# q and k in two float32r parts, paired heads in 64-row groups of TensorE, late maximum tiles by half the keys

## The chip, the cores and the metric

The kernel runs on one core of a Trainium2 chip. The metric is the device time of one launch in microseconds (us), here the median of three runs.

## The reference

Input is x of shape (4, 1024, 128) and float32 weights. Three residual steps follow each other:

```python
x = x + 0.5 * ffn(layernorm(x))       # router over 8 experts, one expert per token, 128 -> 512 -> 128, relu
x = x + attention(layernorm(x))
x = x + 0.5 * ffn(layernorm(x))
# attention: 16 heads of 8 numbers each, causal, 1024 keys
q, k, v = split_heads(x @ Wq.T), split_heads(x @ Wk.T), split_heads(x @ Wv.T)   # (64, 1024, 8)
q, k = rope(q, pos), rope(k, pos)
score = einsum('bqd,bkd->bqk', q, k); score = where(causal, score, -inf)
out = einsum('bqk,bkd->bqd', softmax(score / sqrt(8)), v) @ Wo.T
```

The output is (4, 1024, 128) float32. The change concerns q, k and the scores alone.

## The kernel before, in words

There are two blocks of work. The first holds the first feed-forward step (`ffn`), the projections (`project`) and the attention (`attention`); the second holds the last feed-forward step. Each engine has its own program, in a fixed order, and semaphores join them.

**Projection** (`project`, L849 to L1093). The 4096 tokens go through in 8 groups of 512 (`NC8`). For a group, ScalarE normalises, TensorE turns the tokens (`turn`) and multiplies (`products`): q and k, each with a second product for the rotation by position, 4 products of 512 columns in float32, and the values. VectorE multiplies by cosine and sine (`rotate`), GpSimd adds the two. Then q and k are split in three bfloat16 parts (`KINDS = 3`): ScalarE copies the high part (`hi`, L1003), `subtract_hi` (L912) takes it off, ScalarE copies the middle part (`mid`, L1010), and `subtract_mid` (L920 on VectorE for q, L1047 on GpSimd for k) leaves the low part. SyncE stores the parts to DRAM (`keep`, L1071), 6 DMAs a group.

**Stacks** (`stack_parts`, L809). A stage of the attention is 4 heads (`QH`) of one batch; there are 16 stages (`NST`). For each, q and k are read back into SBUF as stacks of 72 rows: 3 by 3 parts by 8 numbers, arranged so that one bfloat16 product over the 72 rows gives all products of parts. Rows 72 to 74 hold minus the row maximum, in three parts too, against ones. 11 DMAs load one stage's stacks, into a ring of three buffers.

**Stage** (`plan`, L1129). The scores are computed twice. First, in a *tile*, queries are on partitions and keys in the columns, so that VectorE can take the row maximum (`tile` L1297 on TensorE, `reduce` L1439 on VectorE). Tiles of stage s+1 are computed while stage s is weighed. The first half of the queries (blocks 0 to 3) has 8 tiles of two heads by at most 512 keys. The late half (blocks 4 to 7) has 16 tiles of one head by 640 to 1024 keys, two matmuls each. There are two PSUM buffers of 1024 columns for tiles (`psS`). The maxima of a half are split by GpSimd (`split`), turned by TensorE (`turn_max`), copied by VectorE (`copy_max`), and written by one DMA of SyncE (`load_max`, L1269) into the stack's rows. Second, in a *unit*, keys are on partitions: TensorE computes a score per head (`score`, L1326, 128 to 512 queries wide), ScalarE the exponential, GpSimd masks the diagonal block, and TensorE multiplies with the values (`weigh`, L1342: four heads at once, each in 32 columns of the array, in float32). A stage has 12 units: 6 are 512 queries wide, 2 each 384, 256 and 128. Scores have three PSUM buffers (`psST`), so a score waits for the exponential three before it. In the order of TensorE a unit's first score comes before the weighing of two units earlier, then the other scores with tiles spread between them by `tile_cost`. `EXTRAS` (L1192) puts the turn of the late half's maxima after unit 1, while the late half starts with unit 4.

**Opening.** Before the first stage the 24 tiles of stage 0 run by themselves, with the first four units of stage 0 spread among the last of them (`opening`, L1172). `warm_up` runs short products on TensorE before it.

## Time and profile before

| | |
|---|---|
| Median of 3 runs | 913.79 us (913.56 to 918.77) |
| Span of the profiled execution, first to last instruction | 855.6 us |
| Around the span, median less span | 58.2 us |
| TensorE | 779.7 us busy (91%) |
| VectorE | 610.9 us (71%) |
| ScalarE | 507.4 us (59%) |
| GpSimd | 315.4 us (37%) |
| Mean granted clock of TensorE | 0.945 |

The profiled execution's own time outside the span isn't listed, so the 58.2 us set its span beside the median of the runs. A row of the profile names the line of the kernel, the engine, the operation, what it writes and reads with partitions by elements, the count, then busy time and the mean time of one. Busy times of instructions that overlap are counted once; the mean is of the single durations.
### The profile page before, as it was taken

What the parts mean: (1) busy time and instruction counts of PE and PEld (TensorE: products, weight loads), DVE (VectorE), ACT (ScalarE), POOL (GpSimd) and SP (SyncE); (2) the same over time, 40 slices, a digit from 0 to 9 for tenths busy, and PEclk for the clock granted to TensorE, in tenths of its full rate; (3) what the DMA queues carried; (4) which work ended last, traced back from release to release, by engine and by line L of the source; (5) the groups of instructions that cost most, each with busy time, mean ns of one, the idle gap of its engine ahead of it and who ended that gap; (6) DMA issues with size and microseconds to landing.
All of it is one profiled execution on the core that took longest, in us unless ns stands there. A gap on an engine that the chain in (4) does not pass through costs nothing. (4 is left out here: it accounts for less than half of the span.)

```text
span 855.6 us, 17846 instructions
## 1 busy us (share of the span) xinstructions
PE 779.7 (91%) x5570; PEld 427.9 (50%) x5570; DVE 610.9 (71%) x1919; ACT 507.4 (59%) x1229; POOL 315.4 (37%) x603
## 2 busy tenths in 40 slices
PE   9889999887899999999999999999999997689995
PEld 8888896543233333333333333333333335579884
DVE  4657774698668777788878878788787722856663
ACT  2166651673247767667667766766777684146662
POOL 6177742475104223223322422331242231056753
PEclk8699999998569999999999999999999998789998
DMA  8721113065332033033113303312320001122110
GB/s 271 270 57 50 54 33 117 23 169 159 57 57 45 14 57 57 10 49 58 34 26 57 53 6 57 58 22 36 57 41 18 3 1 34 73 70 50 52 42 26
DMA packets 27989, 51.84 MB, mean 61 GB/s; under 512 B 7552, under 2 KB 19200, under 8 KB 26496
## 3 DMA queue, kind: packets, MB, share of 16 engines
q1 hardware_dynamic: 21296, 41.04, 20.7%
q0 software_dynamic: 4096, 8.69, 3.8%
q10 hardware_dynamic: 2512, 1.06, 0.5%
q8 instruction: 43, 0.70, 0.4%
q14 instruction: 42, 0.34, 0.1%
HBM read 35.40 MB, written 14.97 MB: 59 GB/s over the span
## 5 line engine op out<-in xcount | busy, mean ns | idle before, releaser
L1448 DVE CUSTOM_DVE_ANT_0 cst<-psS,mask_row 128x768 bf16<-128x768 f32 (+7 forms) x512 | 364.7, 756 | 100.2 <-PE psS L1308 97.6
L1412 ACT ACTIVATE prob<-psST 128x512 f32<-128x512 f32 (+3 forms) x750 | 317.3, 495 | 158.9 <-PE psST L1339 155.2
L1353 PE MATMUL a_psO<-prob,vs 128*32 128x512 f32 (+3 forms) x1536 | 166.7, 506 | 2.8 <-ACT prob L1412 1.7
L1532 POOL TENSOR_TENSOR a_gate<-a_zeros 1x1 f32<-1x1 f32 x128 | 23.7, 185 | 333.7 <-ACT prob L1412 333.7
L1339 PE MATMUL psST<-a_qs,ks 75*128 75x512 bf16 (+1 forms) x480 | 123.7, 327 | 5.9 <-ACT prob L1412 3.5
L1308 PE MATMUL psS<-ks,a_qs 72*128 72x512 bf16 (+2 forms) x480 | 119.0, 337 | 5.6 <-DVE a_rowmax L1448 5.5
L777 POOL DMA_INDIRECT tok<-rows,f_there_number x64 | 61.8, 966 | 86.0 <-DVE f_number L489 42.0
L1308 PEld LDWEIGHTS psS<-ks,a_qs 72*128 72x128 bf16 x480 | 35.6, 99 | 101.1 <-DVE a_rowmax L1448 33.0
L1308 PE MATMUL psS<-ks,qs 72*128 72x512 bf16 (+3 forms) x288 | 75.8, 354 | 6.7 <-DVE a_rowmax L1448 6.5
L1533 POOL TENSOR_SCALAR_AFFINE_SELECT prob<-prob 128x512 f32<-128x512 f32 x128 | 80.3, 627 | 0.0
L1339 PE MATMUL psST<-qs,ks 75*128 75x512 bf16 (+3 forms) x270 | 73.4, 346 | 2.7 <-ACT prob L1412 1.7
L1339 PEld LDWEIGHTS psST<-a_qs,ks 75*128 75x128 bf16 x480 | 43.8, 97 | 61.4 <-ACT prob L1412 28.8
L726 ACT ACTIVATE f_xnT<-f_ps_half,gb 128x128 f32<-128x128 f32 x64 | 29.3, 458 | 54.4 <-PE f_ps_half L654 54.4
L522 DVE TENSOR_SCALAR f_hidT<-f_ps_wide,f_w1s 128x128 f32<-128x128 f32 x156 | 47.2, 345 | 18.0 <-PE f_ps_logit L663 13.7
L663 PE MATMUL f_ps_wide<-f_xnT,f_w1s 128*128 x312 | 49.7, 282 | 10.0 <-ACT f_hidT L734 5.4
L743 ACT ACTIVATE f_w1s<-w 128x516 f32 x78 | 49.7, 637 | 9.8 <-DVE f_item_ring L479 9.3
L1353 PEld LDWEIGHTS a_psO<-prob,vs 128*32 128x32 f32 x1536 | 30.6, 108 | 48.1 <-ACT prob L1412 31.6
L1308 PEld LDWEIGHTS psS<-ks,qs 72*128 72x128 bf16 x288 | 21.6, 100 | 64.5 <-DVE a_rowmax L1448 28.4
L663 PEld LDWEIGHTS f_ps_wide<-f_xnT,f_w1s 128*128 128x128 f32 x312 | 40.9, 191 | 14.1 <-issue 14.0
L673 PE MATMUL f_ps_rank<-w,f_hidT 128*128 x320 | 45.4, 285 | 0.3 <-DVE f_hidT L522 0.3
L1339 PEld LDWEIGHTS psST<-qs,ks 75*128 75x128 bf16 x270 | 25.6, 102 | 38.8 <-ACT prob L1412 17.9
L1448 DVE DVE_READ_ACCUMULATOR2_ANT a_rowmax<- 128x1 f32 x512 | 42.6, 83 | 0.0
(183 smaller groups left out, 1066.1 us busy)
## 6 DMA issues: line engine op xcount, KB each, us to landing
a_qs<-q_split SPq DMA_DIRECT2D x60, 96.0 KB
rows<-tok SPq DMA_DIRECT2D x8, 536.0 KB, 4.9
ks<-k_split SPq DMA_DIRECT2D x32, 128.0 KB
qs<-q_split SPq DMA_DIRECT2D x36, 96.0 KB
q_split<-p_part SPq DMA_DIRECT2D x24, 128.0 KB, 2.4
k_split<-p_part SPq DMA_DIRECT2D x24, 128.0 KB, 2.4
ks<-k_split SPq DMA_DIRECT2D x16, 192.0 KB
tok<-x_after_first SPq DMA_DIRECT2D x4, 536.0 KB, 5.4
```

What stands on the lines that cost most here:

```text
L522: last = nc.vector.tensor_scalar(hidT[i % 2][:, f * P:(f + 1) * P], hidden_at(i, f), w1s[i % 4][:, F + f:F + f + 1], 0.0, ALU.add, ALU.max)
L663: last = nc.tensor.matmul(hidden_at(i, f), w1s[i % 4][:, f * P:(f + 1) * P], xnT[:, ds(slot_of[i], 1), :], start=True, stop=True)
L673: last = nc.tensor.matmul(psY[i % 2], hidT[i % 2][:, f * P:(f + 1) * P], n.w2[:, ds(expert[i], 1), f * D:(f + 1) * D], start=(f == 0), sto ...
L726: nc.scalar.activation(xnT[:, t % XR, :], psX[t % 2], ACT.Identity, bias=n.gb[:, 1:2], scale=n.gb[:, 0:1]).then_inc(x_ready, 1)
L743: nc.scalar.activation(w1s[i % 4][:, :], n.w1[:, ds(expert[i], 1), :], ACT.Copy).then_inc(w1_ready, 1)
L777: pool.indirect_dma_start(out=row[:, t, :], out_offset=None, in_=n.rows_dram[r][:, :], in_offset=bass.IndirectOffsetOnAxis(ap=there_number ...
L1308: last = nc.tensor.matmul(ps[:, a * CH + c0:a * CH + c0 + w], lhs, ks[r][0:PR, h * S + c0:h * S + c0 + w], start=True, stop=True)
L1339: nc.tensor.matmul(score_buffer(s, m)[:, 0:w], ks[r][:, h * S + j * P:h * S + (j + 1) * P], qs[r][:, q_col(h, q0):q_col(h, q0) + w], start ...
L1353: last = nc.tensor.matmul(psO[32 * h:32 * h + 32, c0:c0 + w], vs[r][:, j, h, :], prob[:, u % RING, h, 0:w], start=(j == 0), stop=(u + 1 in ...
L1412: nc.scalar.activation(prob[:, u % RING, h, 0:w], score_buffer(s, u * QH + h)[:, 0:w], ACT.Exp, scale=SCALE).then_inc(exp_done, 1)
L1448: last = nc.vector.tensor_tensor_reduce(out=out[:, a * CH:a * CH + width], in0=ps[:, a * CH:a * CH + width], in1=mask_row[:, S - width:], ...
L1533: nc.gpsimd.affine_select(out=part, in_=part, compare_op=ALU.is_ge, fill=0.0, base=0, pattern=[[0, QH], [1, P]], channel_multiplier=-1).th ...
```

## The change

q and k are split in two float32r parts in place of three bfloat16 ones. The step of the middle part goes away. A head's 2 by 2 parts by 8 numbers are 32 rows; even heads stand in partitions 0 to 63, odd heads in 64 to 127, each group filled up to 62 rows with zeros (q) against ones (k), and two rows for the maximum. A late tile is now two heads by one half of the keys; its first half is reduced by one `tensor_reduce` for both heads into `early_max`, from which the second half's reduction starts. Each maximum is written by four DMAs in place of one. The weighing comes ahead of the unit's scores, and no tile is put between the first two scores. In the opening, six short products per 512 columns follow each tile that has no units beside it (`idle`).

```diff
-KINDS = 3
-PR = KINDS * KINDS * DK
+KINDS = 2
+SIDES = 2
+SIDE = P // SIDES
 MR = KINDS
+USED = KINDS * KINDS * DK
+PR = SIDE - MR
+SH = QH // SIDES
+IDLE = 6
...
-        n.ks = [sb(f"ks{i}", [PR + MR, QH * S], BF16) for i in range(RING)]
-        n.qs = [sb("qs0", [PR + MR, QH * S], BF16)]
+        n.ks = [sb(f"ks{i}", [P, SH * S], F32R) for i in range(RING)]
+        n.qs = [sb("qs0", [P, SH * S], F32R)]
...
+def spare_rows(a):
+    return slice(a * SIDE + USED, (a + 1) * SIDE)
...
+    for a in range(SIDES):
+        link(nc.gpsimd.memset(n.qs[0][spare_rows(a), :].bitcast(F32), 0.0))
     for r in range(RING):
-        link(nc.gpsimd.memset(n.ks[r][64:PR + MR, :], 1.0))
+        for a in range(SIDES):
+            link(nc.gpsimd.memset(n.ks[r][spare_rows(a), :].bitcast(F32), 1.0))
...
-STACK_DMAS = 2 * KINDS - 1 + KINDS * NCH
+STACK_DMAS = SIDES * (2 * KINDS + 1)
...
+    def heads(source, first, last, a):
+        return source[first * DK:last * DK, ds(s * QH, QH), :].rearrange("d (g a) t -> a d g t", a=SIDES)[a]
+    def rows(stack, a, at, count):
+        here = a * SIDE + at * DK
+        return stack[here:here + count * DK, :].bitcast(F32).rearrange("d (g t) -> d g t", g=SH)
+    for a in range(SIDES):
+        yield rows(k, a, 0, KINDS), heads(n.k_dram, 0, KINDS, a)
+        for c in range(KINDS):
+            yield rows(k, a, KINDS + c, 1), heads(n.k_dram, KINDS - 1 - c, KINDS - c, a)
+        for c in range(KINDS):
+            yield rows(q, a, c * KINDS, KINDS), heads(n.q_dram, 0, KINDS, a)
...
@@ project, VectorE (GpSimd does the same for i = 1)
         def subtract_hi(g, k):
-            for i in range(2):
-                dve.wait_ge(hi_done[i], g + 1)
-                wait(dve, lo_done[i], g - 1)
-                nc.vector.tensor_tensor(rest[i][k], rot[i][k], part[i][k][:, 0, :],
-                                        ALU.subtract).then_inc(rest_done[i], 1)
-        def subtract_mid(g, k):
-            dve.wait_ge(mid_done[0], g + 1)
-            nc.vector.tensor_tensor(part[0][k][:, 2, :], rest[0][k], part[0][k][:, 1, :],
+            dve.wait_ge(hi_done[0], g + 1)
+            nc.vector.tensor_tensor(part[0][k][:, 1, :], rot[0][k], part[0][k][:, 0, :].bitcast(F32),
                                     ALU.subtract).then_inc(lo_done[0], 1)
@@ project, ScalarE
-        def mid(g, k):
-            for i in range(2):
-                act.wait_ge(rest_done[i], g + 1)
-                nc.scalar.activation(part[i][k][:, 1, :], rest[i][k], ACT.Copy).then_inc(mid_done[i], 1)
@@ project, GpSimd
+        clear = Chain(pool, n.rows_cleared)
+        for r in range(1, RING):
+            for a in range(SIDES):
+                clear(nc.gpsimd.memset(n.qs[r][spare_rows(a), :].bitcast(F32), 0.0))
@@ attention
-    tiles += [((h,), i) for i in (CB, TB - 1, CB + 1, TB - 2) for h in range(QH)]
+    tiles += [((h, h + 1), i, c0) for i in (CB, TB - 1, CB + 1, TB - 2) for c0 in (0, CH) for h in range(0, QH, 2)]
...
             w = units[u][3]
+            if u >= (OPEN + LAG if first and not whole else LAG):
+                found.append(("weigh", u - LAG, 0))
...
             for h in range(0 if first and u < OPEN and not whole else QH):
                 found.append(("score", u, h))
                 att += w
-                if h == 0:
-                    if u >= (OPEN + LAG if first and not whole else LAG):
-                        found.append(("weigh", u - LAG, 0))
...
-                spread()
+                if h:
+                    spread()
...
     def q_col(h, q):
-        return (q // CH * QH + h) * CH + q % CH
+        return h // SIDES * S + q
+    def side(h, rows):
+        return slice(h % SIDES * SIDE, h % SIDES * SIDE + rows)
@@ load_max
-            sp.dma_start(max_rows(r, half), maxT[half][:, :]).then_inc(max_loaded[half], 16)
+            for k in range(QH):
+                a, g = k // SH, k % SH
+                sp.dma_start(max_rows(r, half, g * SIDES + a),
+                             maxT[half][k * MR * CB:(k + 1) * MR * CB, :].bitcast(F32)).then_inc(max_loaded[half], 16)
@@ tile and score
+                last = nc.tensor.matmul(ps[:, a * CH:a * CH + w], qs[r][side(h, PR), q_col(h, i * P):q_col(h, i * P) + P],
+                                        ks[r][side(h, PR), q_col(h, c0):q_col(h, c0) + w], start=True, stop=True)
...
+        def idle(times):
+            for _ in range(times):
+                nc.tensor.matmul(psO[:, 0:P], n.onesb[:, :], n.onesb[:, :], start=True, stop=True)
...
+            nc.tensor.matmul(score_buffer(s, m)[:, 0:w], ks[r][side(h, PR + MR), q_col(h, j * P):q_col(h, j * P) + P],
+                             qs[r][side(h, PR + MR), q_col(h, q0):q_col(h, q0) + w],
+                             start=True, stop=True).then_inc(scored, 1)
@@ reduce
+            if i >= CB and c0 == 0:
+                nc.vector.tensor_reduce(early_max[:, :, g, i - CB], ps[:, :].rearrange("p (a w) -> p a w", a=SIDES),
+                                        AX.X, ALU.max).then_inc(use_read, 1)
+                return
             for a, h in enumerate(heads):
+                known = early_max[:, a, g, i - CB:i - CB + 1] if c0 else LOWEST
```

The split of the maxima on GpSimd goes from five operations to three, and the turn of the maxima is in float32.

## Rows read from the trace of the kernel before

**Rows 1.** Page, busy time by engine.

```profile
PE 779.7 (91%) x5570; PEld 427.9 (50%) x5570; DVE 610.9 (71%) x1919; ACT 507.4 (59%) x1229; POOL 315.4 (37%) x603
```

**Rows 2.** Windows: stretch, busy PE, PEld, DVE, ACT, POOL, then clock, DMA share.

```profile
202.30:217.90 15.60, 11.28 (x34) 2.27 (x35) 13.79 (x48) 2.14 (x4) 7.30 (x12) 0.61 0.58 147
217.90:234.00 16.10, 14.86 (x55) 5.13 (x55) 10.83 (x29) 6.12 (x16) 2.95 (x11) 0.50 0.30 46
234.00:264.80 30.80, 29.08 (x145) 9.42 (x144) 21.56 (x57) 14.85 (x33) 4.94 (x15) 0.74 0.23 40
264.80:689.10 424.30, 404.54 (x2828) 148.91 (x2828) 338.40 (x981) 296.64 (x702) 121.17 (x378) 1.00 0.22 38
689.10:713.10 24.00, 21.26 (x169) 6.91 (x169) 1.99 (x7) 20.53 (x53) 7.98 (x23) 1.00 0.01 2
```

**Rows 3.** Timeline of PE, stage in the steady part: start, length.

```profile
401.24 0.60 PE L1308 MATMUL psS<-ks,qs 72*128 72x512 bf16 x2
401.68 0.60 PE L1339 MATMUL psST<-a_qs,ks 75*128 75x512 bf16 x2
...
403.07 1.06 PE L1353 MATMUL a_psO<-prob,vs 128*32 128x512 f32 x8
404.07 0.60 PE L1308 MATMUL psS<-ks,qs 72*128 72x512 bf16 x2
...
418.93 0.43 PE L1353 MATMUL a_psO<-prob,vs 128*32 128x128 f32 x8
419.29 0.39 PE L1308 MATMUL psS<-ks,a_qs 72*128 72x256 bf16 x2
```

**Rows 4.** Timeline of DVE, one wide tile after another.

```profile
401.88 1.23 DVE L1448 CUSTOM_DVE_ANT_0 cst<-psS,mask_row 128x1024 bf16<-128x1024 f32 x1 [1.17 <-PE psS L1308]
...
403.03 1.22 DVE L1448 CUSTOM_DVE_ANT_0 cst<-psS,mask_row 128x1024 bf16<-128x1024 f32 x1
```

**Rows 5.** Lines: DVE, a plain reduction.

```profile
L475 DVE TENSOR_REDUCE f_expert<-f_upto 128x39 f32<-128x312 f32 x2 | 1.0, 478 | 0.1
```

**Rows 6.** Lines: float32 product of 512 columns; weight loads of bfloat16 and float32.

```profile
L957 PE MATMUL psS<-p_anT,wall 128*128 128x512 f32 x64 | 29.0, 595 | 0.7 <-ACT p_anT L992 0.7
L1339 PEld LDWEIGHTS psST<-a_qs,ks 75*128 75x128 bf16 x480 | 43.8, 97 | 61.4 <-ACT prob L1412 28.8 <-issue 8.7
L663 PEld LDWEIGHTS f_ps_wide<-f_xnT,f_w1s 128*128 128x128 f32 x312 | 40.9, 191 | 14.1 <-issue 14.0
```

**Rows 7.** Windows as in rows 2: the opening's first microseconds.

```profile
204.00:206.00 2.00, 1.13 (x6) 0.23 (x4) 2.00 (x11) 1.16 (x2) 1.79 (x2) 0.91 0.44 117
206.00:208.00 2.00, 1.78 (x4) 0.26 (x4) 1.82 (x9) 0.63 (x1) 2.00 (x3) 0.50 0.73 202
```

**Rows 8.** Timeline of a projection group: VectorE, then the next products.

```profile
178.45 3.60 PE L957 MATMUL psS<-p_anT,wall 128*128 128x512 f32 x8
179.30 2.36 DVE L917 TENSOR_TENSOR prob<-prob,p_part 128x512 f32<-128x512 f32 x2
183.98 1.36 DVE L923 TENSOR_TENSOR p_part<-prob,p_part 128x512 bf16<-128x512 f32 x1
184.41 3.60 PE L957 MATMUL psS<-p_anT,wall 128*128 128x512 f32 x8
```

**Rows 9.** Timeline of GpSimd: clearing a stack, and its idle time before the projection.

```profile
0.80 3.50 POOL L244 MEMSET ks<- 11x4096 bf16 x1 [0.29 <-POOLq L1585]
...
152.19 1.27 POOL L1038 TENSOR_TENSOR prob<-prob 128x512 f32<-128x512 f32 x1 [17.15 <-DVE prob L909]
```

**Rows 10.** Timeline: the late maxima's way to the first late score.

```profile
420.63 0.22 PE L1316 MATMUL psS<-identb,a_maxparts 128*128 128x128 bf16 x1
421.67 0.70 SPq L1272 DMA_DIRECT2D qs<-a_maxT  x1
422.42 0.45 SPq L826 DMA_DIRECT2D ks<-k_split  x1
424.77 0.38 PE L1339 MATMUL psST<-qs,ks 75*128 75x512 bf16 x1
```

More of the change, by code:

```diff
@@ L9 @@
 BF16 = mybir.dt.bfloat16
+F32R = mybir.dt.float32r
 U32 = mybir.dt.uint32
@@ L1057, in _ @@
             if g >= 1:
-                subtract_mid(g - 1, (g - 1) % 2, 1)
-        subtract_mid(NC8 - 2, 0, 0)
-        subtract_hi(NC8 - 1, 1)
-        for i in range(2):
-            subtract_mid(NC8 - 1, 1, i)
+                subtract_hi(g - 1, (g - 1) % 2)
+        subtract_hi(NC8 - 1, (NC8 - 1) % 2)
     @block.sync
@@ L1076, in keep @@
                     rows = slice(m * DK, (m + 1) * DK)
-                    if i == 0:
-                        there = n.q_dram[rows, k, heads, :]
-                    else:
-                        there = n.k_dram[rows, heads, k * CH:(k + 1) * CH]
-                    sp.dma_start(there.rearrange("d h t -> h d t"), part[i][k][:, m, :]).then_inc(split_stored[i][k], 16)
+                    there = (n.q_dram, n.k_dram)[i][rows, heads, k * CH:(k + 1) * CH]
+                    sp.dma_start(there.rearrange("d h t -> h d t"), part[i][k][:, m, :].bitcast(F32)).then_inc(split_stored[i][k], 16)
         for g in range(EARLY):
@@ L1114, in attention, with tile_width @@
     half_end = [CB, UN]
-    tiles = [((h, h + 1), i) for i in range(CB) for h in range(0, QH, 2)]
+    tiles = [((h, h + 1), i, 0) for i in range(CB) for h in range(0, QH, 2)]
     HALF_TILES = len(tiles)
-    tiles += [((h,), i) for i in (CB, TB - 1, CB + 1, TB - 2) for h in range(QH)]
+    tiles += [((h, h + 1), i, c0) for i in (CB, TB - 1, CB + 1, TB - 2) for c0 in (0, CH) for h in range(0, QH, 2)]
     MT = len(tiles)
-    tile_cost = [len(heads) * (i + 1) * P + 350 for heads, i in tiles]
+    def tile_width(t):
+        _, i, c0 = tiles[t]
+        return min((i + 1) * P - c0, CH)
+    tile_cost = [len(tiles[t][0]) * tile_width(t) + 350 for t in range(MT)]
     tile_total = sum(tile_cost)
@@ L1151, in plan @@
             w = units[u][3]
+            if u >= (OPEN + LAG if first and not whole else LAG):
+                found.append(("weigh", u - LAG, 0))
+                att += WEIGH_COST * units[u - LAG][3]
+            elif u < LAG and not first:
+                found.append(("weigh", u - LAG, 1))
+                att += WEIGH_COST * units[u - LAG + UN][3]
             for h in range(0 if first and u < OPEN and not whole else QH):
@@ L1217, in sem @@
         return ctx.enter_context(nc.semaphore(f"a_{name}"))
-    qs = n.qs + [sb(f"qs{i}", [PR + MR, QH * S], BF16) for i in range(1, RING)]
+    qs = n.qs
     ks, vs = n.ks, n.vs
@@ L1244, in attention, with max_rows @@
     max_loaded = [sem(f"max_loaded{i}") for i in range(2)]
-    def max_rows(r, half):
-        return qs[r][PR:PR + MR, half * QH * CH:(half + 1) * QH * CH]
+    def max_rows(r, half, h):
+        rows = slice(h % SIDES * SIDE + PR, h % SIDES * SIDE + PR + MR)
+        return qs[r][rows, q_col(h, half * CH):q_col(h, half * CH) + CH].bitcast(F32)
     def run(stage):
@@ L1297, in tile @@
         def tile(r, turn, t, index, ps):
-            heads, i = tiles[t]
+            heads, i, c0 = tiles[t]
             if t == 0:
@@ L1393, in _ @@
                 tile(0, 0, arg, k, psS[k % 2])
+                if alone:
+                    idle(IDLE * tile_width(arg) // CH)
                 k += 1
@@ L1502, in split @@
             wait(pool, maxT_ready, 2 * s + half)
-            src = rowmax[:, :, half * CB:(half + 1) * CB]
-            done = order * 4
+            src = rowmax[:, :, :, half * CB:(half + 1) * CB]
+            done = order * 2
             def link(ins, k):
```

110 lines of the change are left out of this document (41 added, 69 removed).

## The prediction

> **What bounds the kernel now.** I read the page's busy times first: TensorE is busy for 91% of the span, more than any other engine [rows 1]. A share over the whole span hides stages with different limits, so the windows come next [rows 2]. From 264.8 to 689.1 us run 14 stages of the attention, 424.3 us or 30.3 us each. Per stage TensorE is busy 404.54 / 14 = 28.9 us, VectorE 24.2, ScalarE 21.2. The granted clock is 1.00, the 2.4 GHz level. So half of the span is one repeated stage, bound by TensorE, with VectorE 4.7 us behind. The opening before it (202.3 to 234.0 us) is different: VectorE is busy 24.6 of 31.7 us, and the clock stands at 0.61 and then 0.50.
>
> The timeline of TensorE says what a stage's 28.9 us are [rows 3]. Two products of 512 columns start 0.44 us before the next two. A stage has 4608 query-by-key columns a head, for 4 heads 18,432 columns of tiles and as many of scores: 18 times 0.44 = 7.9 us each. A weighing takes 1.00 us at 512 columns (403.07 to 404.07) and 0.36 us at 128; on the straight line between, 0.79 and 0.57 us at 384 and 256. The 12 of a stage cost 6 x 1.00 + 2 x (0.79 + 0.57 + 0.36) = 9.4 us. That is 25.2 us; the turns of maxima and outputs and what lies between groups make the other 3.7.
>
> **Tiles and scores on TensorE.** The columns stay the same in number. What changes is their price: float32r for bfloat16, and two heads side by side in halves of the array. No row shows float32r. The near ends are the bfloat16 product, 0.22 us per 512 columns [rows 3], and the float32 one, whose two records take 29.0 / 64 = 0.45 us each, 0.91 us together [rows 6]. I take the bfloat16 price: q and k come in two rounded parts, and the operation leaves nothing over for a second part inside the product. No row shows row groups either, but column groups are shown: a weighing is 8 float32 records of 512 columns in 1.00 us [rows 3], where 8 such records on the whole array take 3.60 us [rows 8]. Narrow groups do run side by side there. If pairs do, tiles and scores cost 7.9 us together, not 15.8, and TensorE is busy 28.9 - 7.9 = 21.0 us a stage. The ends: nothing gained (pairs one after another), and 15.8 us lost (float32 price, two halves in parallel, 31.5 us).
>
> The Trainium skill, "TensorE: Matmul & The Clock Gate", Part 3, states that matmuls in different row groups overlap, measured 3.07 times for four. By that page two groups would come near the factor 2 of the sum; no run here shows it yet.
>
> **VectorE becomes the next limit.** Elements stay equal: a late pair of heads was two reductions and is one plain reduction of 1024 plus two shorter ones. So 8 operations a stage are added. One wide tile starts 1.15 us after another [rows 4] for a length of 1.23; a plain reduction of 312 elements takes 0.478 us [rows 5]. A line through both lengths is 1.05 ns an element and 0.15 us fixed. Of the fixed part about 0.08 us shows between starts (1.23 - 1.15 overlap). The 8 cost between 0.6 and 1.2 us; I take 0.6, since they overlap in these rows. VectorE then needs 24.2 + 0.6 = 24.8 us a stage.
>
> ScalarE is not far: the last stage has no tiles, and even so takes 24.0 us, with ScalarE busy 20.5 [rows 2]. That chain of score, exponential and weighing is a floor too, for all stages. A stage therefore ends between 24.8 us and 30.3. The engine that bounds now stands still 1.4 us a stage. VectorE has only two tile buffers ahead of it and will stand still longer: I take 2.0 us, so 26.8 us. Gain 3.5 us x 14 = 49 us; with 1 to 3.5 us of standing, 63 to 28 us.
>
> **The new order.** The weighing ahead of the first score delays that score by up to 1.00 us [rows 3]. Behind it wait ScalarE and, through the queue of TensorE, the next tile. Three PSUM buffers leave ScalarE up to two or three exponentials to do meanwhile, which is the cover; I price it at nothing here, it is in the 2.0 us. In return the first two scores stand next to each other and can pair. The third and fourth can be parted by a tile, and then pair less well; that costs up to 0.2 us in some units.
>
> **Opening and first stage.** The idle products are there to be run beside VectorE's work. In the window before the clock fell TensorE was busy 1.13 of 2.0 us [rows 7], after it at 0.50. Should it stay at 1.00, the opening falls to VectorE's 24.6 us plus its waits, some 28 us: 4 us saved, between 0 and 7. Stage 0 falls from 30.8 us like the others: 3.5 us, 0 to 6.
>
> **Projection.** A group starts 5.96 us after the one before (178.45 to 184.41), paced by VectorE [rows 8]. Gone are one of its two high subtractions (half of 2.36 us) and the middle one (1.36). TensorE's products are 3.60 us of a group, turns and values come on top, so it is next, with the stores behind it. Between 0 and 2.36 us a group are to be had; I take 0.9, 7 us in 8 groups. Stores grow from 6 x 128 KB to 4 x 256 KB a group, in longer pieces. On GpSimd 8 clearings of 2048 float32 replace 3 of 3.50 us [rows 9]; at 1.75 to 3.5 us each, 14 to 28 us against 10.5, before any token is fetched. Four more (7 to 14 us) lie ahead of the projection, under 17.15 us of idle time. Both at nothing. If that cover were gone, the excess comes on top, some 10 us at most.
>
> **Sum.** 49 + 4 + 3.5 + 7 = 63.5 us. Span 855.6 - 63.5 = 792. The span lies 58.2 us under the median of the runs, and I keep that distance: 913.8 - 63.5 = **850 us**. The likeliest case by itself: 825 to 880 us.
>
> **Rivals.**
>
> *The maxima come late.* From the issue of the DMA at 421.67 to the first late score at 424.77 are 3.1 us, and the next issue follows 0.75 us later [rows 10]. Three more issues add up to 2.2 us, and the units between get some 0.4 us shorter. The landing isn't shown; if it had 1.6 us to spare, TensorE stops 1 us before each late half, tiles run out behind it, and 15 us come on top: 865 us (888 without any slack). For it: the only path that gets longer. Against: three operations replace five on GpSimd.
>
> *The pair saves nothing.* Each product brings its own weight load. It takes 97 ns in bfloat16 and 191 ns in float32 [rows 6]. Two loads of 191 ns after each other are 0.38 us, more than a pair's 0.22; 48 pairs would cost 18.3 us instead of 7.9, TensorE 31.4 us, and a stage 31 to 32: 913 to 930 us. Half of that cost, or row groups that don't overlap, leave the stage at about 28.5 to 30.3 us and the gains outside it: 875 to 899. I put this case at 900. Against it: in [rows 3] loads disappear behind products.
>
> The Trainium skill, same page, "Weight-path perf modes", says that the fast weight load needs an input that is not float32. The rows agree in direction, 191 against 97 ns; what float32r gets, neither row nor page says.
>
> *The clock falls (the slower side).* TensorE would be busy 21 of 26.8 us in every stage. The rows show the clock at 1.00 through the last stage (21.26 of 24.0 us busy) and falling to 0.50 in the opening, where products waited for VectorE [rows 2, 7]. At half clock weighings, scores and tiles cost 2 x 17.3 = 34.6 us, with the 3.7 left 38.3 a stage. With a share x of the stages there, a stage takes 26.8 + 11.5 x; above x = 0.4 that eats all other gains too. At one half: 32.5 us, 31 us more, less 11 saved elsewhere: 934 us. Place: any steady stage. Against it: at half clock TensorE would be busy without a break, and from such a stretch it came back between 234.0 and 264.8 us (0.74, then 1.00) [rows 2].
>
> *float32r is not what it seems.* At twice the price of bfloat16 the pair just makes up: 899 us. At the float32 price, 15.8 + 21.0 + 7.9 = 44.7 us a stage, over 1100.
>
> **How the numbers follow.** Chances: forecast 0.55 (850), late maxima 0.12 (865), no saving from pairs 0.13 (900), clock 0.13 (934), dear float32r 0.07, about half of it beyond 1000. The range must leave out no more than 2 in 10. Its low end, 815, is the forecast with 1 us of standing still and the full gains outside the stages; its high end, 920, takes in the case without savings and leaves out most of the clock case and the dearest float32r. A measurement of this kernel can tell about 1% from no change, 904.7 to 922.9 us. Faster by more: the forecast, the late maxima and 0.05 of the pairs' case, 0.72. Within: 0.06 of the pairs' case, 0.03 of the dear product at twice the price, and 0.02 of the clock's, 0.11. Slower: what is left of the three, 0.17.
>
> **What would show it.** Two neighbouring products of tiles or scores start 0.22 us apart but end together, or their pair starts 0.22 us before the next pair: pairs overlap. If the starts keep 0.22 us within the pair too, they don't. PEld records at 97 or 191 ns decide on the loads. VectorE over 90% busy in the steady stages, with waits for tiles under 2.5 us a stage, shows the new limit. The clock in the windows should be 1.00 from the opening on. A wait of TensorE ahead of the first late score, longer than before, shows the late maxima. Steady stages above 28.5 us make the forecast wrong; so does a clock below 1.00 in them.

## The result, and the profile after

The kernel became slower: 950.52 us against 913.79 us in the median, ratio 1.041 with a 95% interval of 1.036 to 1.045. The forecast was 850 us. Runs over 1.5% above the fastest of their kernel are left out of every ratio below, though not out of the medians, and two traces (old order, shorter reduction) are of such runs.

First the total. I had set the profiled span of before, 855.6 us, beside a median of 913.8 and kept the distance of 58.2 us. That distance is no time around the span. It lies in the two feed-forward steps, which the change doesn't touch. Windows of before, then of another execution of the same kernel (stretch, busy PE, PEld, DVE, ACT, POOL, clock, DMA share):

```profile
0.00:130.80 130.80, 120.34 (x982) 111.63 (x983) 87.29 (x351) 64.61 (x164) 74.41 (x75) 0.92 0.39 121
717.90:855.60 137.70, 114.24 (x939) 105.33 (x939) 86.51 (x353) 62.98 (x160) 62.83 (x64) 0.91 0.18 54
```

```profile
0.00:164.30 164.30, 134.34 (x982) 123.79 (x983) 87.57 (x351) 64.63 (x164) 74.09 (x75) 0.82 0.31 96
297.53:721.91 424.38, 404.52 (x2832) 148.93 (x2828) 338.45 (x981) 296.72 (x700) 121.14 (x379) 1.00 0.22 38
750.20:917.00 166.80, 123.56 (x939) 114.11 (x939) 86.97 (x353) 63.04 (x160) 62.65 (x64) 0.84 0.15 44
```

Both feed-forward steps took 33.5 and 29.1 us more in the second execution, and its 14 steady stages the same 424.4 us as in [rows 2]. Every later run, of either kernel, looks like the second. So the middle between the two steps is what can be compared (before: the first of the two executions):

| us | before | after | forecast of the change |
|---|---|---|---|
| projection | 54.9 | 48.3 | -7 |
| opening and stage 0 | 63.0 | 63.9 | -7.5 |
| stages 1 to 14 | 424.4 | 466.3 | -49 |
| last stage | 28.3 | 29.7 | 0 |
| the middle, with 16.7 of warm-up | 587.1 | 624.9 | -63.5 |

Cut points are the first product of the warm-up, the first turn of the projection, the first tile, the first exponential of stages 1 and 15, and the first turn of the second feed-forward step. The middle grew by 37.8 us, the medians by 36.7. The second execution of before has 56.4, 60.2, 424.4 and 28.3 us in these rows, 585.9 in all: the steady stages repeat, projection and opening move by up to 3 us from one execution to the next.

The page of after, busy time by engine; then windows: the end of the projection, the opening with its low clock, three single steady stages, all 14, and the last.

```profile
PE 817.9 (85%) x5642; PEld 497.1 (52%) x5642; DVE 625.0 (65%) x2035; ACT 494.3 (52%) x1213; POOL 308.0 (32%) x544
```

```profile
219.00:235.30 16.30, 16.04 (x132) 10.31 (x130) 10.64 (x32) 5.18 (x14) 10.50 (x9) 1.00 0.96 299
235.30:279.70 44.40, 41.25 (x192) 21.01 (x190) 33.42 (x102) 10.73 (x25) 5.39 (x18) 0.50 0.37 54
295.94:327.64 31.70, 28.40 (x204) 12.55 (x204) 25.74 (x78) 20.92 (x51) 7.78 (x24) 1.00 0.26 36
327.64:360.88 33.24, 29.89 (x204) 12.93 (x204) 25.78 (x78) 20.92 (x50) 7.77 (x24) 0.95 0.24 34
620.83:659.60 38.77, 36.40 (x204) 15.98 (x204) 25.91 (x78) 21.14 (x50) 7.77 (x24) 0.74 0.21 29
295.94:762.28 466.34, 420.43 (x2828) 184.67 (x2828) 361.02 (x1092) 293.49 (x701) 108.93 (x323) 0.94 0.22 31
762.28:791.98 29.70, 20.89 (x164) 8.11 (x164) 1.93 (x7) 20.71 (x51) 6.85 (x20) 0.94 0.01 2
```

Against [rows 2]: VectorE needs 25.8 us a stage (24.2 before), ScalarE 21.0, TensorE 28.4 in a stage at full clock (28.9 before; the forecast was 21.0), and no engine fills the stage. Two things made the stages longer. The first is the clock: 1.00 before, it has stretches at 0.50, five of 3.4 us and two of 20.5 us. A stage with a short one takes 33.0 to 33.3 us, with a long one 38.8 to 39.1. The second is there without it: the seven stages without any such stretch take 31.8 us on average, 1.53 more than before. So of the 41.9 us, 14 x 1.53 = 21 are there at full clock, and the other 21 come with the clock. From here on "undisturbed" means the mean of the stages that no stretch at 0.50 touches.

What the pairs do is in the timeline of after, products first, then weight loads (start, length; neighbours of one line are grouped with their count; rows left out between the last two loads):

```profile
405.12 0.43 PE L1364 MATMUL a_psO<-prob,vs 128*32 128x128 f32 x8
405.47 0.50 PE L1349 MATMUL psST<-qs,ks 64*128 64x512 f32 x2
405.81 0.45 PE L1313 MATMUL psS<-ks,qs 62*128 62x512 f32 x4
406.10 0.44 PE L1349 MATMUL psST<-qs,ks 64*128 64x512 f32 x1
407.52 0.33 PE L1313 MATMUL psS<-ks,qs 62*128 62x128 f32 x2 [0.99 <-DVE a_early_max L1463]
407.69 0.45 PE L1349 MATMUL psST<-qs,ks 64*128 64x512 f32 x1
```

```profile
405.47 0.19 PEld L1349 LDWEIGHTS psST<-qs,ks 64*128 64x128 f32 x2 [0.20 <-issue]
405.58 0.47 PEld L1313 LDWEIGHTS psS<-ks,qs 62*128 62x128 f32 x4
406.04 0.18 PEld L1349 LDWEIGHTS psST<-qs,ks 64*128 64x128 f32 x1
409.65 0.19 PEld L1349 LDWEIGHTS psST<-qs,ks 64*128 64x128 f32 x2 [0.84 <-ACT prob L1426]
```

Two scores share one row of 0.50 us: their single records start 3 ns apart, as do the two heads of a tile. So pairs do overlap, where [rows 3] had 0.22 us for each product. But a load takes 0.19 us, as in float32 [rows 6], and where one has waited for its buffer, its product's record begins with it. The record is then longer by the load, and the mean length of a product of 512 columns shows how often that happens (steady stages of before, of after, and of after with bfloat16, which is an experiment below):

```profile
L1339 PE MATMUL psST<-a_qs,ks 75*128 75x512 bf16 x240 | 78.2, 380 | 4.7 <-ACT prob L1412 3.5
```

```profile
L1349 PE MATMUL psST<-qs,ks 64*128 64x512 f32 x337 | 120.4, 491 | 4.3 <-ACT prob L1426 3.3
L1313 PE MATMUL psS<-ks,qs 62*128 62x512 f32 x336 | 75.9, 438 | 0.0
```

```profile
L1349 PE MATMUL psST<-qs,ks 64*128 64x512 bf16 x337 | 95.6, 383 | 7.1 <-ACT prob L1426 4.4
L1313 PE MATMUL psS<-ks,qs 62*128 62x512 bf16 x336 | 65.1, 379 | 1.7
```

A score takes 491 ns, not 380 (469 in the undisturbed stages alone, with a load of 183 ns; the rest is the low clock). Not all products pair: of a stage's 96 products of tiles and scores, 34 start within 20 ns of the one before. Who waits for whom shows in the waits of one stage, before and after (total, times, longest):

```profile
ACT prob L1412 <- PE psST L1339: 8.4, 12, 1.3
PEld psST L1339 <- ACT prob L1412: 2.9, 8, 0.6
```

```profile
ACT prob L1426 <- PE psST L1349: 11.3, 12, 1.5
PEld psST L1349 <- ACT prob L1426: 11.2, 20, 0.8
```

ScalarE waits for a score once in each of the 12 units, 8.4 us a stage before and 11.3 after, and the loads of scores wait for exponentials, 2.9 and 11.2 us. The two engines stand in a loop of score, exponential, weighing and back. That ScalarE's work and waits add up to about the stage (21.2 + 8.4 = 29.6 of 30.3) names no limit: this is so for every engine. Followed back through the 14 stages from each instruction to what released it, as the page does it for the whole span, some 75% of the time before lies in TensorE's products, 15% in VectorE's reductions and 5% in exponentials; after, 72, 11 and 12%. This is a rough estimate, since the ends of products are modelled.

In the Trainium skill, "TensorE: Matmul & The Clock Gate", Part 3 says that products in different row groups overlap. The 3 ns agree. "Weight-path perf modes", on the same page of the Trainium skill, keeps the fast load for inputs that are not float32. Float32r's 193 to 196 ns against 94 to 98 for bfloat16 put float32r with float32 here.

### The profile page after: what moved, and what is told of

It is laid out like the page before. It is cut to its first block and busy times, and to the rows that moved or that the text cites. A ratio compares the mean times of both kernels' runs of the same rounds, so it can differ in the third digit from the quotient of the medians.

```text
span 958.7 us, 18083 instructions
## 1 busy us (share of the span) xinstructions
PE 817.9 (85%) x5642; PEld 497.1 (52%) x5642; DVE 625.0 (65%) x2035; ACT 494.3 (52%) x1213; POOL 308.0 (32%) x544
## 5 line engine op out<-in xcount | busy, mean ns | idle before, releaser
L1349 PE MATMUL psST<-qs,ks 64*128 64x512 f32 (+3 forms) x750 | 236.6, 438 | 18.5 <-ACT prob L1426 15.2
L1349 PEld LDWEIGHTS psST<-qs,ks 64*128 64x128 f32 x750 | 110.4, 196 | 200.5 <-ACT prob L1426 160.0
L1463 DVE TENSOR_REDUCE a_early_max<-psS 128x2 f32<-128x1024 f32 x128 | 153.9, 1223 | 53.0 <-PE psS L1313 51.1
L1313 PE MATMUL psS<-ks,qs 62*128 62x512 f32 (+3 forms) x768 | 158.0, 404 | 23.8 <-DVE a_early_max L1463 19.1
L1468 DVE CUSTOM_DVE_ANT_0 cst<-psS,mask_row 128x128 bf16<-128x128 f32 (+3 forms) x256 | 112.0, 489 | 48.5 <-PE psS L1313 47.3
L1468 DVE CUSTOM_DVE_ANT_0 cst<-psS,mask_row,a_early_max 128x128 bf16<-128x128 f32 (+3 forms) x256 | 127.2, 547 | 6.2 <-PE psS L1313 5.0
L1313 PEld LDWEIGHTS psS<-ks,qs 62*128 62x128 f32 x768 | 90.2, 203 | 57.8 <-DVE a_early_max L1463 33.3
L1364 PEld LDWEIGHTS a_psO<-prob,vs 128*32 128x32 f32 x1536 | 31.3, 111 | 40.7 <-ACT prob L1426 28.3
L804 POOL DMA_INDIRECT x_after_first<-tok,f_there_number x32 | 31.9, 997 | 47.5 <-DVE tok L567 40.8
L687 PE MATMUL f_ps_number<-w,f_hidT 128*128 x304 | 45.5, 297 | 0.0
L804 POOL DMA_INDIRECT out_x<-tok,f_number x32 | 31.9, 997 | 41.4 <-DVE tok L559 24.1
```

The lines of the kernel that those rows point to most:

```text
L687: last = nc.tensor.matmul(psY[i % 2], hidT[i % 2][:, f * P:(f + 1) * P], n.w2[:, ds(expert[i], 1), f * D:(f + 1) * D], start=(f == 0), sto ...
L804: pool.indirect_dma_start(out=target, out_offset=bass.IndirectOffsetOnAxis(ap=number[:, t:t + 1], axis=0), in_=row[:, t, 0:TW if r == 0 el ...
L1313: last = nc.tensor.matmul(ps[:, a * CH:a * CH + w], qs[r][side(h, PR), q_col(h, i * P):q_col(h, i * P) + P], ks[r][side(h, PR), q_col(h, c ...
L1349: nc.tensor.matmul(score_buffer(s, m)[:, 0:w], ks[r][side(h, PR + MR), q_col(h, j * P):q_col(h, j * P) + P], qs[r][side(h, PR + MR), q_col ...
L1364: last = nc.tensor.matmul(psO[32 * h:32 * h + 32, c0:c0 + w], vs[r][:, j, h, :], prob[:, u % RING, h, 0:w], start=(j == 0), stop=(u + 1 in ...
L1463: nc.vector.tensor_reduce(early_max[:, :, g, i - CB], ps[:, :].rearrange("p (a w) -> p a w", a=SIDES), AX.X, ALU.max).then_inc(use_read, 1)
```

## The experiments

Each ratio is to the kernel before, run beside the changed one. What an experiment leaves out is said in the text put on record for it.

**Before again.** The kernel before as it was, executed once more.

> The kernel before, unchanged, run and profiled once more. In its first profiled execution the span was 855.6 us, 58 us under the timed median, while the changed kernel's span lies only 1.8 us under its time. Theory A: the timed runs hold time in the two feed-forward steps that the first trace of the kernel before did not have, and a second trace will have a span near 912 us with the attention from the warm-up to the last output at the same 587 us. Theory B: 58 us lie around the span in this kernel, and the span will be near 856 us again.

918.72 us, with the windows shown above. The distance is feed-forward time, as theory A had it.

**The order of the weighing**, in both kernels. The weighing behind the second score (first run) and, as before, behind the first, with a tile allowed there (second run); then the kernel before with the weighing first.

```diff
-            if u >= ...: found.append(("weigh", u - LAG, 0))
             for h in range(...):
                 found.append(("score", u, h))
+                if h == 1:           # second run: h == 0, and spread() after every score
+                    if u >= ...: found.append(("weigh", u - LAG, 0))
                 if h:
                     spread()
```

> The changed kernel with the weighing put behind the second score of a unit, so that the first two scores still pair. Theory order (the weighing ahead of all scores starves ScalarE for 1.4 us a unit): ScalarE's idle time falls, stages go from 33.3 us to 27 to 29 us, time 870 to 900 us. Rival VectorE (its reductions and the two tile buffers set the pace whatever the order): stages stay at 31 to 33 us, time within 10 us of 950. Rival clock: any gain of order is taken back by more stretches at 1.2 GHz, 930 us or more.

> The changed kernel with the order of before: first score, weighing, three scores, tiles allowed after each score. Theory order: ScalarE is fed during the weighing by one exponential instead of two, so stages of 28 to 30.5 us, 880 to 910 us. Rival VectorE: as e2, within 10 us of 950. If pairing the first two scores matters, this one is slower than the kernel with two scores ahead of the weighing by up to 0.2 us a unit, 35 us.

> The kernel before with only the new order (weighing ahead of the unit's scores, no tile after the first score). Theory order: ScalarE starves here as well, 0.5 to 1.5 us a stage more than 30.3, 920 to 940 us. Rival (the order is harmless, the loss comes from the tiles or from the clock): 914 us within 5.

Ratios 1.049 (1.043 to 1.055), 1.054 (1.048 to 1.059) and 1.012 (1.008 to 1.016). In the kernel before, the weighing first costs 1.08 us a stage (30.31 to 31.39, all 14 alike) at a clock of 1.00: ScalarE waits 10.1 us in place of 8.4. In the changed kernel it is the other way: undisturbed 31.84 with the weighing first, 32.21 behind the second score (two stages only) and 32.53 in the old order (five stages). Both moves in the changed kernel were expected to gain, and both lost. So the order is no cause by itself; what it is worth depends on the rest of the kernel.

**Four short filler products** before each tile, in a stage.

```diff
+            if adding:                        # sums open in psO
+                for _ in range(4):
+                    nc.tensor.matmul(psO[0:32, 0:P], zero_weights, n.onesb[:, :], start=False, stop=False)
             use(index)
```

> The changed kernel, with four short bfloat16 products (128 columns, zero weights, added into the output sums, so nothing changes in them) before each tile of a stage that finds the sums open, 18 or so of 24. They run where TensorE would wait for a tile buffer. Theory C (the stretches at 0.50 cost 21 of the 42 us that the 14 stages grew by, and they come where TensorE has waited): no low stretch is left in the steady stages, and these fall from 466 to about 446 us (31.8 each), some 930 us in all. Theory C2 (the clock does not matter, the low stretches lie where TensorE waits anyway): stages stay at 466 or grow by the products' own time, up to 18 x 0.25 = 4.5 us a stage. Theory N (the low stretches come whatever TensorE does): the clock row is as before, time about 950 to 960.

They could be placed before 16 of the 24 tiles. 1014.2 us, ratio 1.107 (1.102 to 1.112). The undisturbed stage went from 31.84 to 36.11 us. It has 64 fillers of 0.06 us from start to start, 3.8 us: all of it, and more, came out at the end. TensorE's own order of work has no slack, although it waits. And ten stretches of 3.4 us at 0.50 stayed. Theory C failed in this form; the growth is the one of theory C2.

**VectorE relieved**: a shorter plain reduction.

```diff
-  nc.vector.tensor_reduce(early_max[...], ps[:, :].rearrange("p (a w) -> p a w", a=SIDES), AX.X, ALU.max)
+  nc.vector.tensor_reduce(early_max[...], ps[:, :].rearrange("p (a w) -> p a w", a=SIDES)[:, :, 0:P], AX.X, ALU.max)
```

> The changed kernel, in which VectorE's plain reduction of a late tile's first half of keys reads 128 of 512 columns a head (left out: the other 384, so the maximum is over fewer keys). It takes 8 x 0.75 = some 6 us of VectorE's 25.8 away per stage and leaves TensorE and ScalarE alone. Theory V (VectorE with its two tile buffers sets the undisturbed stage of 31.8 us): the stage falls by 3 us or more, to under 29; in all 905 or less. Theory K (the stage is set by the chain score, exponential, weighing and the waits of TensorE's own queue; VectorE has time to spare, 6 us a stage): the stage stays within 1 us of 31.8, in all 940 to 955.

922.45 us, ratio 1.002 (0.997 to 1.007). VectorE has 6.1 us less to do, the undisturbed stage fell by 1.4, to 30.42. Neither expectation held: VectorE takes part, through the two tile buffers that TensorE waits for, but a quarter of its work gone gives 1.4 us, so it isn't the limit by itself.

**Whole-key tiles** in the changed kernel, then with the old order as well.

```diff
-    tiles += [((h, h + 1), i, c0) for i in (CB, TB - 1, CB + 1, TB - 2) for c0 in (0, CH) for h in range(0, QH, 2)]
+    tiles += [((h,), i, 0) for i in (CB, TB - 1, CB + 1, TB - 2) for h in range(QH)]
...        (two products a tile, and no plain reduction)
```

> The changed kernel, with the late tiles as they were: one head by all of its 640 to 1024 keys, two products on the same half of the array, one reduction. Two-part float32r, paired scores and the weighing first stay. Theory T (the new late tiles cost the stage: 8 more operations, the maxima as operand, 1.6 us of VectorE): VectorE falls back to 24.2 us and the undisturbed stage from 31.8 to about 30.5; in all some 930. Theory P (pairs matter most): 16 tiles lose their overlap, 16 x up to 0.2 = 3 us more of TensorE, stage 33 or more, but the clock stays at 1.00.

> As the run before, and the weighing again behind the unit's first score. What is left of the change is the two parts in float32r, the halves of the array (scores and first tiles side by side) and the four maximum DMAs. If late tiles and order are what costs (theory T with O): stage at 30.3 or below, in all under 913.8, about 905 with the projection's gain. If the float32r products and their longer weight loads cost (theory L: 196 for 97 ns, exposed where a score waits for its buffer): stage at 31 to 32 again, about 930.

943.26 us (1.033, 1.028 to 1.038), undisturbed 31.45; and 982.46 us (1.068, 1.062 to 1.075), 33.13 (two stages). The second has the order and the tile form of before and is 2.8 us a stage slower at full clock. What still differs are float32r in two parts, the halves of the array and the maximum's four DMAs. That pointed to float32r.

**The tile form alone, in the kernel before**; and **bfloat16 in the changed kernel**.

```diff
-        n.ks = [sb(f"ks{i}", [P, SH * S], F32R) for i in range(RING)]
+        n.ks = [sb(f"ks{i}", [P, SH * S], BF16) for i in range(RING)]
...        (the same for qs, the parts, their DRAM copies and the parts of the maxima)
```

> The kernel before (three bfloat16 parts, one stack of 72 rows, old order) with one edit: the late tiles are two heads by one half of the keys, reduced by one plain reduction and then two that start from its maximum. Theory T (this tile form costs a stage by itself, as the whole-key run suggests with 0.4 us): stage 30.31 to 30.6 or 31; VectorE 24.2 to 25.8 us. Theory S (TensorE's own sequence sets the stage, VectorE's time does not matter): stage within 0.2 us of 30.31. The clock should stay at 1.00 under both; if it falls, it is the tile form that lets it fall, and neither float32r nor the pairs.

> The changed kernel with bfloat16 in place of float32r for the two parts (left out: what the second bfloat16 part leaves over, so q and k are less exact); halves of the array, pairs, tiles and order stay. Theory L (each product brings a float32r weight load of 183 to 196 ns, which stands open between a tile and a score, and eats what the pairs save): loads fall to some 100 ns, some 36 crossings between tiles and scores at 0.07 to 0.09 us each make 3 us, and the undisturbed stage falls from 31.8 to about 28.5 to 29.5; in all 880 to 900. Theory R (the order of waits between the engines sets the stage, not the loads): stage within 0.7 us of 31.8. For the clock: if float32r lets it fall, it stays at 1.00 here; if pairs and waits do, it falls as often or more.

Tile form: 925.27 us (1.013, 1.010 to 1.017), stage 31.03, so 0.72 us. The clock stays at 1.00. bfloat16: 891.17 us (0.977, 0.974 to 0.979), stage 29.44 against 31.84, and no stretch at 0.50 in the 14 stages:

```profile
282.23:694.39 412.16, 348.05 (x2827) 101.19 (x2827) 354.19 (x1093) 291.21 (x700) 108.86 (x323) 1.00 0.07 18
```

512 columns keep their price; what changes on TensorE are the loads, 94 for 196 ns, and its busy time falls from 28.4 to 24.9 us a stage. Theory L holds: 2.4 us a stage. The share of the loads alone isn't shown, since the stacks' bytes are halved too and the maxima are turned in bfloat16.

**No idle products** in the opening (`IDLE = 0`).

> The changed kernel without the short idle products of the opening. If they hold the clock up there at all, opening and first stage get longer than 63.9 us (by 2 us or more) with a longer stretch at 0.50. If they only stand in TensorE's queue, the stretch gets shorter by up to 2 us or stays.

Opening and stage 0 took 61.1 us, not 63.9, with 41.0 us at 0.50 in place of 44.4. So the idle products had not held the clock up. Whether they cost the 2.8 us isn't shown: it is a single execution, and the kernel before has 63.0 and 60.2 us there in two.

**A version for both**: three bfloat16 parts, but only the six products of parts with a share (48 rows and three for the maximum), so a head fits in half of the array. Then with the rows filled up by zeros to 61 and 64, as in the changed kernel.

```diff
-KINDS = 2
+KINDS = 3
-USED = KINDS * KINDS * DK
-PR = SIDE - MR
+USED = KINDS * (KINDS + 1) // 2 * DK
+PR = USED                                   # zero rows: PR = SIDE - MR
...        (bfloat16 as above)
+        for at, c in ((0, 0), (KINDS, 1), (2 * KINDS - 1, 2)):
+            yield rows(k, a, at, KINDS - c), heads(n.k_dram, c, KINDS, a)       # k's parts in reverse
+            yield rows(q, a, at, KINDS - c), heads(n.q_dram, 0, KINDS - c, a)
```

> A version for both: three bfloat16 parts as before, but only the six products of parts that matter (48 rows and three for the maximum), so that a head fits in a half of the array; pairs, half-key tiles and the weighing first as in the changed kernel, projection as before. Theory L: loads of some 100 ns and pairs together, stage 28.5 to 29.5, projection 55 to 56 us, in all 885 to 905, faster than both. Theory R: stage about 31.8, in all about 940.

> The paired version with three bfloat16 parts, with its 48 rows filled up to 61 by zeros and the maximum above them, as the changed kernel does it. If the rows at work decide on the clock, the one stretch at 0.50 in each stage goes and the stage is 29.4 in place of 30.7 us, some 895 in all. If not, 30.7 and 910 as before.

912.73 us (1.002, 0.999 to 1.005), with thirteen stretches of 3.4 us at 0.50, one in each stage but the first, 30.7 us apart; and 903.41 us (0.989, 0.984 to 0.993), with two stretches in 14 stages. Undisturbed both take 29.4 us (the first in its only such stage). The 14 stages of the first and of the second:

```profile
287.76:716.40 428.64, 367.81 (x2827) 105.86 (x2827) 354.43 (x1093) 291.31 (x700) 121.86 (x379) 0.95 0.14 26
```

```profile
288.95:702.49 413.54, 352.06 (x2827) 101.48 (x2827) 354.60 (x1093) 291.34 (x700) 121.68 (x379) 0.99 0.15 27
```

The difference are rows that add zero, and the clearing of them. All ten executions of the first have a granted clock of 0.889 to 0.903 over the whole kernel, all five of the second 0.912 to 0.926. The two were not run beside each other; the kernel before took 911.1 and 914.6 us beside them. A fall in the first version, in windows of 2 us, lies where TensorE waited for VectorE (busy 1.07 of 2.0 us):

```profile
388.00:390.00 2.00, 1.87 (x20) 0.84 (x19) 1.48 (x4) 2.00 (x5) 1.05 (x5) 1.00 0.79 118
390.00:392.00 2.00, 1.07 (x5) 0.56 (x6) 1.96 (x9) 1.52 (x4) 0.00 (x0) 0.71 0.78 101
392.00:394.00 2.00, 2.00 (x12) 0.48 (x10) 0.55 (x2) 0.28 (x1) 0.00 (x0) 0.50 0.35 43
```

**Pairs alone, VectorE relieved without long loads, whole-key tiles with three parts.** The first is the version with three parts in the old order and with whole-key tiles; the second the one with two bfloat16 parts and the shorter reduction; the third the version with three parts, the weighing first and whole-key tiles.

> Three bfloat16 parts in 48 rows, heads in halves of the array, but whole-key tiles and the old order: the pairs (first tiles and the scores that stand next to each other) are nearly all that is left of the change. By the prediction's step TensorE would fall from 28.9 us to well under 25 (8 first tiles and half of the scores pair, 2 to 4 us) and the stage with it, to 27 or 28. By the chain theory (exponentials, one weighing and the queue in front of them set the stage; a pair only shortens what is waited for elsewhere) the stage stays between 29.8 and 30.3.

> The changed kernel in bfloat16, with VectorE's plain reduction cut to 128 of 512 columns (left out: the other keys of that half, and what two bfloat16 parts leave over). It takes 6 us of VectorE's 25.3 per stage. If VectorE is the next limit behind the loads, as the prediction had it, the stage falls from 29.4 to under 27.5; if the chain of TensorE and ScalarE is, to no less than 28.5. With float32r the same edit gave 1.4 us.

> The paired version with three bfloat16 parts and the weighing first, but whole-key tiles. The tile form was worth 0.4 us with float32r and 0.7 in the old kernel: undisturbed stage 28.7 to 29.1 us. TensorE waits less for VectorE's wide first reduction, ahead of which the stretch at 0.50 began; if that wait is its cause, the clock stays at 1.00 and the whole takes 890 or less, faster than both kernels. If not, 30 us a stage and 905.

Pairs alone: 947.5 us (1.037, 1.033 to 1.042). The undisturbed stage is 30.91 us, no shorter than the 30.31 of before (two stages only), and 88.7 us of the 14 ran at 0.50. Such a stage:

```profile
325.06:355.97 30.91, 24.74 (x206) 7.87 (x202) 24.03 (x71) 21.05 (x51) 8.62 (x28) 1.00 0.16 28
```

TensorE is busy 24.7 us, 4.2 less than before, and the stage has not become shorter. One wait is new in it, for the four DMAs of the late maxima. At 1.1 us it is more than the 0.6 that the stage grew by, so that the pairs without it might gain some 0.5. In the undisturbed stages of the changed kernel none shows:

```profile
333.59 0.39 PE L1372 MATMUL psST<-qs,ks 51*128 51x512 bf16 x1 [1.09 <-DMA qs<-a_maxT]
```

VectorE relieved: 872.87 us (0.958, 0.953 to 0.963), stage 28.07, again 1.4 less for 6 us less work, and again between the two expectations; four stretches of 3.4 us at 0.50. It leaves out a part of the maximum, so it is no candidate. Whole-key tiles: 905.1 us (0.991, 0.988 to 0.994), undisturbed 28.94, but two stretches of 17.1 us at 0.50.

**The best of both, and the order once more.** The same with zero rows, with the weighing first and then behind the second score.

> Three bfloat16 parts, paired, rows filled up with zeros, the weighing first, whole-key tiles. If the zero rows hold the clock whatever the tiles are: 28.9 us a stage, no stretch at 0.50, some 893 to 897 us. If what they did was chance of phase, low stretches as with e19 (34 us of them), 905.

> The same, with the weighing behind the unit's second score. Behind two paired scores the exponentials have work during the weighing. If that cover matters, the undisturbed stage falls by up to 1 us, to 28; with float32r the same move had made it 0.4 us longer (31.84 to 32.21), and if TensorE's sequence decides, it does so here: 29.3.

889.42 us, ratio 0.976 (0.971 to 0.982): faster than both kernels, with three parts. Undisturbed 28.94, one stretch of 3.4 us at 0.50, and a granted clock of 0.921 to 0.929 in its executions, where the same without zero rows had 0.903 to 0.910:

```profile
287.08:693.42 406.34, 357.58 (x2827) 108.77 (x2827) 336.57 (x981) 292.24 (x700) 121.18 (x379) 1.00 0.15 27
```

The second: 923.47 us (1.014, 1.008 to 1.020), undisturbed 31.32. The place of the weighing is worth 2.4 us a stage here, against my expectation of at most 1, and with the other sign than I had for a gain. Some 0.9 us of it is the wait for the DMAs of the late maxima, which this order brings back. In one stage of each, ScalarE's wait for scores:

```profile
ACT prob L1455 <- PE psST L1378: 7.7, 11, 1.2
```

```profile
ACT prob L1456 <- PE psST L1379: 9.1, 13, 1.1
```

With the weighing first, 11 of a stage's 48 scores start within 20 ns of the score before; with the old order 4 (pairs alone), behind the second score 7. In the changed kernel the same counts are 11, 7 and 12, and there the 12 is the longer stage too (32.21 against 31.84). So the number of paired scores doesn't explain what the order is worth.

From before to after, the undisturbed stage goes this way, each step between two runs. Steps under 0.2 us say little: the changed kernel has 31.84 us in one execution and, without the idle products of its opening, 31.68 in another.

```
30.31  before
30.91  pairs, three bfloat16 parts in 48 rows           +0.60
28.94  weighing first (with zero rows the same 28.94)   -1.97
29.37  half-key tiles                                   +0.43
29.44  two parts                                        +0.07
31.84  float32r for bfloat16                            +2.40
```

A step holds where it stands in this row and not by itself: the order alone costs 1.08 us in the kernel before. The other half of the 41.9 us is the clock.

## Why the prediction was wrong

- **TensorE at 21.0 us a stage, VectorE next, stage 26.8 us.** This is the step that failed, twice over. The pairs that form do overlap, as said. But TensorE was busy 28.4 us in an undisturbed stage, not 21.0. With bfloat16 it is 24.9, so pairs took off 4.0 of the 7.9 us, with 34 of 96 products side by side, and float32r put 3.5 back. And I took TensorE's busy time for the limit, and what pairs save in it for time of the stage. Pairs alone took 4.2 us off TensorE and gave a stage 0.6 us longer, with a new wait of 1.1 us for a DMA in it, not 3.5 shorter. At full clock the busy time of neither engine is the limit: 6 us less work for VectorE gives 1.4, yet 3.8 us added to TensorE's queue cost 4.3. What fits all of these is a stage set by the waits between TensorE, ScalarE and VectorE in their fixed orders. Which of them ends last isn't shown step by step, and what less work for ScalarE would give wasn't tried. I had seen that "chain of score, exponential and weighing", and put it at 24.0 us from the last stage, where no tile stands in TensorE's queue.
- **The bfloat16 price for float32r.** Right for the columns (two products of 512 in 0.23 us), wrong for the weight load, 0.19 us; float32r for bfloat16 came to 2.4 us a stage. I had it as a rival ("Each product brings its own weight load"), with 31 to 32 us for the stage. Measured 31.8, by another sum, so the agreement is luck: the loads of a pair don't follow each other (both start within 4 ns), they stand open where a product has waited.
- **The new order, priced at nothing.** Alone in the old kernel it costs 1.08 us a stage; against the old order in a kernel with pairs it gains 0.7 (the changed kernel), 1.7 (with whole-key tiles) and 2.0 (with three bfloat16 parts as well). Both signs were possible, and neither was in the sum.
- **VectorE's 24.8 us.** Measured 25.8. Most of the 1.0 is a term that I did not have: a reduction that starts from `early_max` has a mean of 547 ns, at the same widths one that doesn't has 489, and there are 16 a stage.
- **The clock.** The forecast held it at 1.00; the rival had a share x at the low level and 934 us. It fell in seven stages for 58 us in all, a share of 0.12, and cost 21 us. Its price was near (11.5 x 0.12 x 14 = 20 us). Rival clock and rival loads came together, which no case of mine did: 900 and 934 were each short of 950. The range ended at 920.
- **Opening and first stage, -7.5 us.** Measured +0.9, and +3.7 against the second execution of before. The idle products did not hold the clock: 0.50 from 235.3 to 279.7 us, 44.4 us as before.
- **Projection, -7 us.** Measured -6.6, and -8.1 against the second execution of before. That the 7 was near is partly luck: a group starts 4.80 us after the one before (197.69 to 202.49) in place of 5.96 [rows 8], 1.2 us and not 0.9, but not in all eight groups.
- **Late maxima.** No wait for them shows in the steady stages of after; the rival's mechanism, at its price of 1 us, came up where the weighing stands behind a score: 1.1 us with pairs alone, 0.9 behind the second score, 0.3 on average in the changed kernel with either of these orders. GpSimd's clearings cost nothing that shows.
- **850 from 792.** The 58.2 us were feed-forward time of one quick execution; kept as a difference, they did no harm.
- **Dear float32r.** A slip without effect: 72 products of 512 columns at 0.91 us [rows 6], in two halves side by side, are 32.8 us and not 31.5.

What stays open: why the granted clock falls. Waits alone don't settle it. The kernel with fillers has ten stretches, the one with two bfloat16 parts and longer waits has none, and before the fall at 395.7 us in after TensorE was busy 1.86, 1.83 and 1.75 us in three windows of 2 us. The data type alone doesn't either: with two bfloat16 parts and the shorter reduction there are four stretches. In two pairs of runs zero rows cut the low time from 44.4 to 6.8 and from 34.1 to 3.4 us. That pairs in the old order would gain 0.5 us without the wait for the maxima is a difference of two numbers, and wasn't tried.

## What to carry to other kernels

The busiest engine of a loop isn't always its bound, even at 95%: what an edit takes off its busy time need not come off the period. Nor does a sum of an engine's work and waits name the bound, since it is the period for every engine. Shorten or lengthen one engine's work at a time and see how much of it the period gives back. Two products in halves of the array cost one where both can start together, but each brings its load, and a load behind a semaphore can be on the path: count the products that pair and those that wait, and take bfloat16 where a third part fits in the rows. Test an order again after every change to what it orders; its sign can turn.

## What the runs showed of the hardware

- float32r: columns at the price of bfloat16 (pairs of 512 columns every 0.23 us, 0.22 a product in bfloat16), weight loads at that of float32 (193 to 196 against 94 to 98 ns).
- With rows filled up by zeros the granted clock fell less often: 13 stretches at 0.50 with 51 rows, 2 with 64, same times at full clock. The changed kernel has such rows too, and its clock fell in seven stages.
- One kernel's feed-forward steps took 268.5 us in one execution and 331.1 in another, at clocks of 0.92 and 0.83 on average.
